# Two attention layers and two feed forward layers on one core: the key matrix's low part in device memory, all key projection units from rounded matmuls

## What is computed

```python
x = x + L0_xattn(layernorm(x), ctx)   # 1024 positions of 128 channels, 64 wide queries and keys
x = x + L0_ffn(layernorm(x))          # 1024 x 1024 matrix of signs, scales from a router of 8
# L1_xattn(layernorm(x), ctx): the one whose keys the change touches
Q = einsum('btx,dx->btd', text, Wq) + bq
K = einsum('bpx,dx->bpd', features, Wk) + bk
scores = einsum('btd,bpd->btp', Q, K) / sqrt(1024)
x = x + softmax(scores) @ features
x = x + L1_ffn(layernorm(x))          # 8 low rank pairs, weighed by a router
```

## Time and profile before

| | |
|---|---|
| median of 3 runs | 2312.98 us (2312.54 to 2313.57) |
| the profiled execution | 2312.58 us |
| its span, first to last instruction | 2310.7 us |
| PE, DVE, ACT, POOL busy | 2193.5, 1872.3, 1116.4, 259.9 us |
| mean granted TensorE clock | 0.981 of full |
| DMA | 115.58 MB, 50 GB/s in the mean |

### The profile page before, as it was taken

The page is one execution under the profiler, slowest core; times in us unless marked ns, Lnnn a source line. Parts: engine busy times, 40 slices in busy tenths (PEclk is TensorE's granted clock), DMA queues, the critical chain, the costliest instruction groups (busy, mean ns, idle before and its releaser), DMA issues.

```text
span 2310.7 us, 34120 instructions
## 1 busy us (share of the span) xinstructions
PE 2193.5 (95%) x11166; PEld 1672.1 (72%) x11166; DVE 1872.3 (81%) x3130; ACT 1116.4 (48%) x1657; POOL 259.9 (11%) x302
## 2 busy tenths in 40 slices
PE   1997999999999999999999999999999999999995
PEld 1785677777777777777777777777777777777764
DVE  1435889888888888988888888888888888898883
ACT  1103455555545545555555555555555554555541
POOL 0000111111111111111111111111111111111100
PEclk7899999999999999999999999999999999999997
DMA  8001111111111111111111111111111111111100
GB/s 243 10 1 46 46 37 55 54 54 36 54 45 45 54 53 37 54 54 38 52 54 45 45 54 36 54 54 54 36 54 45 45 54 54 36 54 54 41 23 28
DMA packets 50217, 115.58 MB, mean 50 GB/s; under 512 B 14800, under 2 KB 23248, under 8 KB 50192
## 3 DMA queue, kind: packets, MB, share of 16 engines
q1 hardware_dynamic: 38624, 113.26, 14.9%
q10 hardware_dynamic: 11568, 1.98, 0.6%
HBM read 81.67 MB, written 16.78 MB: 43 GB/s over the span
## 4 chain that ended last, share of the span: by engine, by line
PE 77%; DVE 9%; issue 3%; ACT 2%; POOL 0%; DMA 0%; DVEq 0%; SPq 0%; POOLq 0%; ACTq 0%
PE acc L1091 15%; PE acc L1052 10%; PE scores L1035 5%; PE shared L1065 5%; PE shared L1066 5%; PE scores L1080 5%; PE scores L1079 5%; PE shared L1015 4%; PE shared L1182 3%; PE shared L1166 3%; PE scores L1193 2%; PE scores L1187 2%; DVE x L813 2%; DVE prob L812 2%; PE acc L1048 2%
## 5 line engine op out<-in xcount | busy, mean ns | idle before, releaser
L903 DVE TENSOR_TENSOR p_lo<-prob,p_hi 128x1024 fp32r<-128x1024 f32 x256 | 312.4, 1220 | 106.3 <-ACT p_hi L709 88.4
L702 ACT ACTIVATE prob<-scores 128x1024 f32<-128x1024 f32 x256 | 260.6, 1018 | 228.9 <-PE scores L1080 177.7
L796 DVE TENSOR_REDUCE neg_max<-scores 128x1 f32<-128x1024 f32 x256 | 312.6, 1221 | 38.7 <-PE scores L1035 33.7
L617 POOL TENSOR_TENSOR rstd<-var_eps,minus_half 128x1 f32<-128x1 f32 x128 | 126.9, 991 | 1865.2 <-DVE var_eps L790 1865.2
L709 ACT ACTIVATE p_hi<-prob 128x1024 fp32r<-128x1024 f32 x256 | 271.4, 1060 | 42.8 <-PE acc L1091 38.6
L1052 PE MATMUL acc<-m_whole,cT_whole 128*128 128x512 f32 x512 | 255.9, 602 | 0.0
L911 DVE TENSOR_TENSOR p_sum<-p_sum,prob 128x1024 f32<-128x1024 f32 x192 | 234.1, 1219 | 0.0
L1065 PE MATMUL shared<-signT,y_hi 128*128 128x512 f32 x512 | 206.1, 403 | 0.4 <-ACT oscale L691 0.4
L1079 PE MATMUL scores<-q_hl,k_hh 128*128 128x512 f32 x512 | 201.4, 393 | 1.8 <-DVE q_m L885 1.4
L1066 PE MATMUL shared<-signT,y_lo 128*128 128x512 f32 x512 | 202.4, 395 | 0.0
L1035 PE MATMUL scores<-k_hh,q_hl 128*128 128x512 f32 x512 | 201.9, 475 | 0.3 <-issue 0.3
(11 more groups left out here) (221 smaller groups left out, 4309.8 us busy)
## 6 DMA issues: line engine op xcount, KB each, us to landing
c_in<-in_ctx SPq DMA_DIRECT2D x32, 512.0 KB, 3.3
xn<-in_x SPq DMA_DIRECT2D x32, 512.0 KB, 4.1
x<-in_x SPq DMA_DIRECT2D x32, 512.0 KB, 3.3
c_val<-in_ctx SPq DMA_DIRECT2D x32, 512.0 KB, 3.5
out_x<-oscale SPq DMA_DIRECT2D x32, 512.0 KB, 2.8
q_m<-q_hl SPq DMA_DIRECT2D x32, 256.0 KB, 3.1
k_hh<-k_hh SPq DMA_DIRECT2D x32, 256.0 KB, 3.4
wq_nat<-in_L_xattn_Wq SPq DMA_DIRECT2D x4, 1024.0 KB, 9.9
```

The lines of the kernel that those rows point to most:

```text
L702: nc.scalar.activation(prob[s % 2][:, :], scores[s % 2][:, :], ACT.Exp).then_inc(exp_ready, 1)
L796: nc.vector.tensor_reduce(neg_max[:, t:t + 1], scores[t % 2][:, :], AX_X, ALU.max, negate=True).then_inc(row_max, 1)
L903: nc.vector.tensor_tensor(p_lo[s % 2][:, :], prob[s % 2][:, :], p_hi[s % 2][:, :].bitcast(F32), ALU.subtract).then_inc(p_lo_ready, 1)
```

## The change

M is held as high and low parts for all 8 tiles. The high part stays in SBUF (m_hi, now 8 tiles). The low part is written to device memory (m_low, 16 pieces of 128 x 512, 256 KB each) during the setup, and in every pass SyncE reads the 16 pieces back into a ring of 8 (m_ring). Every unit is three rounded matmuls, in the order hi x hi, lo x hi, hi x low piece, the last of which waits for its piece; each unit raises kw_unit_done, which frees a slot of the ring and takes the place of kw_done. The context is split in both halves: cT_hi and cT_lo for 8 tiles, cT_whole is gone.

The memory is laid out anew: low parts of tiles 4 to 7 are staged in the not yet written tiles 0 to 3 of m_hi, those of tiles 0 to 3 in m_lo_last, gate_parts shares memory with attn.

The order in a pass changes too: the transposes of c_in stand ahead of weigh_values(7), the transposes of xn_3 ahead of both values; ScalarE makes cT_hi twice, then both norm halves, then both den_rows halves; VectorE makes cT_lo in two halves. On SyncE the pieces 12 to 15 of a and 0 to 7 of b stand ahead of c_in, the pieces 8 to 11 of b ahead of the output store.

```diff
-        m_hi = sb("m_hi", [P, TS, D], F32R)
-        m_whole = sb("m_whole", [P, T - TS, D])
+        m_hi = sb("m_hi", [P, T, D], F32R)
...
-        m_lo = sb("m_lo", [P, TS, D], F32R)
+        with ExitStack() as before:
+            m_lo_last = sb("m_lo_last", [P, TS, D], F32R, before)
+        SLOTS = 8
+        m_ring = sb("m_ring", [P, SLOTS, HALF], F32R)
+        m_low = nc.dram_tensor("m_low", [2 * T, P, HALF], F32, kind="Internal").ap()
...
+            def low_stage(ft, cols):
+                return m_lo_last[:, ft, cols] if ft < TS else m_hi[:, ft - TS, cols]
...
+                    for n, (kind, i) in enumerate(groups):
+                        if kind == "m":
+                            ft, h = f_order[i // 2], i % 2
+                            sp.wait_ge(copied, sum(g[0] != "sign" for g in groups[:n + 1]))
+                            sp.dma_start(m_low[h * T + ft],
+                                         low_stage(ft, slice(h * HALF, (h + 1) * HALF)).bitcast(F32)).then_inc(m_stored[ft], 16)
+                    for ft in range(T):
+                        sp.wait_ge(m_stored[ft], 2 * 16)
...
-                            if ft < TS:
-                                nc.vector.tensor_copy(m_hi[:, ft, cols], s[:, :]).then_inc(m_hi_made, 1)
-                                dve.wait_ge(m_hi_made, 2 * ft + i % 2 + 1)
-                                last = nc.vector.tensor_tensor(m_lo[:, ft, cols], s[:, :], m_hi[:, ft, cols].bitcast(F32), ALU.subtract)
-                            else:
-                                last = nc.vector.tensor_copy(m_whole[:, ft - TS, cols], s[:, :])
+                            if ft < TS and i % 2 == 0:
+                                dve.wait_ge(m_stored[ft + TS], 2 * 16)
+                            nc.vector.tensor_copy(m_hi[:, ft, cols], s[:, :]).then_inc(m_hi_made, 1)
+                            dve.wait_ge(m_hi_made, i + 1)
+                            last = nc.vector.tensor_tensor(low_stage(ft, cols), s[:, :], m_hi[:, ft, cols].bitcast(F32), ALU.subtract)
...
+                def low_unit(u):
+                    sp.dma_start(m_ring[:, u % SLOTS, :].bitcast(F32), m_low[u]).then_inc(m_loaded[u % SLOTS], 16)
...
+                    if attend:
+                        for u in range(12, 16):
+                            sp.wait_ge(kw_unit_done, nth(16, a, u - SLOTS + 1))
+                            low_unit(u)
+                    if prepare:
+                        for u in range(SLOTS):
+                            if attend:
+                                sp.wait_ge(kw_unit_done, nth(16, a, u + SLOTS + 1))
+                            low_unit(u)
...
+                    if prepare:
+                        for u in range(8, 12):
+                            sp.wait_ge(kw_unit_done, nth(16, b, u - SLOTS + 1))
+                            low_unit(u)
...
+                    if prepare:
+                        act.wait_ge(cT_done, nth(2, b, 1))
+                        act.wait_ge(kw_unit_done, nth(16, b - 1, 16))
+                        nc.scalar.activation(tile4(cT_hi, 0), shared[0][:, :], ACT.Identity).then_inc(cT_hi_ready, 1)
+                        act.wait_ge(cT_done, nth(2, b, 2))
+                        nc.scalar.activation(tile4(cT_hi, 1), shared[1][:, :], ACT.Identity).then_inc(cT_hi_ready, 1)
                     if chain:
                         act.wait_ge(den_done, nth(1, a, 1))
                         normalize_half(3, c, 0, xn_3, res)
+                        normalize_half(3, c, 1, xn_3, res)
                     if attend:
                         evict_den(a, 0)
...
-                        dve.wait_ge(cT_hi_ready, nth(1, b, 1))
-                        nc.vector.tensor_tensor(cT_lo[:, :, :].rearrange("p t c -> p (t c)"), shared[0][:, :],
-                                                cT_hi[:, :, :].rearrange("p t c -> p (t c)").bitcast(F32),
-                                                ALU.subtract).then_inc(cT_lo_ready, 1)
+                        for h in range(2):
+                            dve.wait_ge(cT_hi_ready, nth(2, b, h + 1))
+                            nc.vector.tensor_tensor(tile4(cT_lo, h), shared[h][:, :], tile4(cT_hi, h).bitcast(F32),
+                                                    ALU.subtract).then_inc(cT_lo_ready, 1)
...
-                        if f < TS:
-                            mm(acc[:, half(h)], cT_hi[:, f, :], m_hi[:, f, half(h)], start=f == 0, stop=False)
-                            mm(acc[:, half(h)], cT_hi[:, f, :], m_lo[:, f, half(h)], start=False, stop=False)
-                            last = mm(acc[:, half(h)], cT_lo[:, f, :], m_hi[:, f, half(h)], start=False, stop=f == T - 1)
-                        else:
-                            last = mm(acc[:, half(h)], cT_whole[:, f - TS, :], m_whole[:, f - TS, half(h)],
-                                      start=f == 0, stop=f == T - 1)
-                        if f == T - 1:
-                            last.then_inc(kw_done, 1)
+                        mm(acc[:, half(h)], cT_hi[:, f, :], m_hi[:, f, half(h)], start=f == 0, stop=False)
+                        mm(acc[:, half(h)], cT_lo[:, f, :], m_hi[:, f, half(h)], start=False, stop=False)
+                        pe.wait_ge(m_loaded[u % SLOTS], nth(32, a, 16 * (u // SLOTS + 1)))
+                        mm(acc[:, half(h)], cT_hi[:, f, :], m_ring[:, u % SLOTS, :], start=False,
+                           stop=f == T - 1).then_inc(kw_unit_done, 1)
...
+                        if prepare and s == 7:
+                            for h in range(2):
+                                pe.wait_ge(x3_ready, nth(2, c, h + 1))
+                                transposes(h, c_in, cT_done)
                         if attend:
                             weigh_values(a, s)
...
-                    if prepare:
+                    if chain:
                         for h in range(2):
-                            pe.wait_ge(x3_ready, nth(2, c, h + 1))
-                            transposes(h, c_in, cT_done)
+                            pe.wait_ge(normed[3], nth(2, c, h + 1))
+                            pe.wait_ge(cT_lo_ready, nth(2, b, h + 1))
+                            transposes(h, xn_3, xnT_done[3])
                     if prepare:
                         pe.wait_ge(normed[0], nth(1, b, 1))
                         values(0, a)
-                    if chain:
-                        for h in range(2):
-                            pe.wait_ge(normed[3], nth(2, c, h + 1))
-                            pe.wait_ge((cT_lo_ready, cT_whole_ready)[h], nth(1, b, 1))
-                            transposes(h, xn_3, xnT_done[3])
-                    if prepare:
                         values(1, a)
```

More of the change, by code:

```diff
@@ L87, in build @@
             wf_first = sb("wf_first", [P, TS, D], F32, before)
-        m_hi = sb("m_hi", [P, TS, D], F32R)
-        m_whole = sb("m_whole", [P, T - TS, D])
-        wf_last = m_whole
+            wf_last = sb("wf_last", [P, T - TS, D], F32, before)
+        m_hi = sb("m_hi", [P, T, D], F32R)
         with ExitStack() as before:
@@ L156, in build @@
             b_hi_made = sem("b_hi_made", tmp)
+            m_stored = [sem(f"m_stored{i}", tmp) for i in range(T)]
+            def low_stage(ft, cols):
+                return m_lo_last[:, ft, cols] if ft < TS else m_hi[:, ft - TS, cols]
             groups = ([("sign", i) for i in range(T)] + [("low", 0), ("low", 1), ("b", 0), ("b", 1)]
@@ L404, in build @@
         k_l1 = sb("k_l1", [P, D], F32R)
-        cT_hi = sb("cT_hi", [P, TS, P], F32R)
-        cT_lo = sb("cT_lo", [P, TS, P], F32R)
-        cT_whole = sb("cT_whole", [P, T - TS, P])
+        cT_hi = sb("cT_hi", [P, T, P], F32R)
+        cT_lo = sb("cT_lo", [P, T, P], F32R)
         neg_max = sb("neg_max", [P, T])
@@ L449, in build @@
         attn = sb("attn", [P, P])
+        gate_parts = attn
         attnT = sb("attnT", [P, P])
@@ L479, in build @@
         maxscores_done = sem("maxscores_done")
-        kw_done = sem("kw_done")
+        kw_unit_done = sem("kw_unit_done")
+        m_loaded = [sem(f"m_loaded{i}") for i in range(SLOTS)]
         max_turned = sem("max_turned")
@@ L503, in build @@
         cT_lo_ready = sem("cT_lo_ready")
-        cT_whole_ready = sem("cT_whole_ready")
         k_hi_ready = sem("k_hi_ready")
@@ L678, in body @@
                     if attend:
-                        act.wait_ge(kw_done, nth(2, a, 1))
+                        act.wait_ge(kw_unit_done, nth(16, a, 8))
                         act.wait_ge(biased, nth(1, a - 1, 1))
@@ L737, in body @@
                         normalize_half(3, c, 0, xn_3, res)
+                        normalize_half(3, c, 1, xn_3, res)
                     if attend:
                         evict_den(a, 0)
-                    if prepare:
-                        act.wait_ge(cT_done, nth(2, b, 1))
-                        act.wait_ge(kw_done, nth(2, b - 1, 2))
```

(9 more changed lines are left out.)

9 lines of the change are left out of this document (3 added, 6 removed).

## The result

The changed kernel takes 2287.32 us (median of four, 2286.79 to 2289.61); the kernel before, run beside it, takes 2313.28 (2312.54 to 2315.55). The ratio is 0.9888, 95% interval 0.9872 to 0.9904. The forecast was 2288. The profiled execution was the longest of the four, 2289.61 us with a span of 2287.8, against 2312.58 and 2310.7 before.

A forecast was written before the change was run, and what follows sets the result against it. TensorE was taken to set most of the period, VectorE to bound wherever it never idles. 2312.6 - 29.0 (31 x 0.49 + 30 x 0.46) - 1.8 (period 1) + 6.3 (start) = 2288 us; range 2270 to 2306.

The forecast's parts named there:

- Units 5 to 7, 0.49 us: Maximum stage: these three rewritten units, 0.163 us each, bring VectorE's row maxima forward, gaining 0.49 us per period.
- Units 4 and 12 to 15, nothing: Maximum stage: 0.82 us of TensorE saved per period behind a busy VectorE becomes waiting and gains nothing.
- Rival A: All TensorE savings count, 1.31 us per period, because VectorE follows; 2263 us, chance 0.07.
- Handover, 0.46 us: End of a period: the new orders let VectorE's x1_half start earlier, gaining 0.46 us in each of 30 periods.
- B: Handover brings nothing: ScalarE's queue is later than worked out and x1_half stays put; 2302 us, chance 0.14.
- C: Neither gain shows and only the start is paid; 2317 us, about no change, chance 0.05.
- D: Handover gets later as work put ahead on ScalarE delays x1_half; 2323 us at 0.7 us later, chance 0.06.
- The cover of the added subtraction: Handover: VectorE's second cT_lo hides in 1.39 us of vanishing idle time; uncovered it would cost 0.69 us per period.
- Transfers, waits and increments, nothing: Every period: 4.2 MB more reads, added waits and unit increments cost 0; other end for waits 0.3 us per period.
- E: The 4.2 MB more per period written into SBUF slow TensorE's matmuls; 2328 us at 2%, chance 0.03.
- G: Pieces arrive late and units wait for them; 2350 us at 2 us late, chance 0.02.
- F: Added waits and increments on TensorE cost their bound, 0.3 us per period; 2297 us, chance 0.05.

The follow-up runs named there:

- full_567: Changed kernel with units 5, 6 and 7 each as one full-precision matmul of the high parts, low parts left out; 2304.25 us, ratio 0.9971.
- Full_rest: Changed kernel with units 4 and 12 to 15 each as one full-precision matmul of the high parts, low parts left out; 2293.76 us, ratio 0.9921.
- experiment 4: Two variants of the changed kernel: units 14 and 15 alone, or 4, 12 and 13 alone, as one full-precision matmul each; 2288.91 and 2290.22 us.
- order_only: Kernel before with only the new handover orders on TensorE and ScalarE; units, memory and transfers as before; 2301.54 us, ratio 0.9957.
- old_order: Changed kernel with the handover orders of the kernel before on TensorE and ScalarE; 2336.97 us, ratio 1.011.
- after_again: Changed kernel, unchanged, run again on the chip of no_pieces and late_start; 2289.13 us, ratio 0.9899.
- no_pieces: Changed kernel without piece loads or their waits, the third matmul reading the high part instead; 2281.14 us, ratio 0.9862.
- late_start: Changed kernel with the first eight pieces issued behind the first c_in and xn, not ahead; 2281.92 us, ratio 0.9867.
- full_4_12_13: Changed kernel with units 4, 12 and 13 each as one full-precision matmul of the high parts, low parts left out; 2290.22 us, ratio 0.9905.
- den_between: late_start with ScalarE copying the first denominator half between the two norm halves, not behind both; 2274.67 us, ratio 0.9833.

## Why the prediction was right, and where its terms were off

- **Units 5 to 7, 0.49 us: right.** full_567 gives 0.49, and the price of a unit, 0.163 us, with it. One thing expected of the profile was not so: the idle time before r_max shrank to 0.20 us and did not go.
- **Units 4 and 12 to 15, nothing: mis-sized, 0.15 us per period, 4.6 us.** The step that failed is "From 1039.71 on it never idles. So units 12 to 15 ... bring nothing". That VectorE never idles shows that nothing holds it up. It does not show that nothing else ends later. The rows that say so, the transpose of the maxima 1.71 us behind the start of TensorE's last two units and with no wait before it, were in the trace of before. Full_rest showed it, and experiment 4 that no one group of units does it: TensorE had 0.33 us to spare at the stage's end, and with all five it is 0.2 us over. Rival A, all 0.82 us, is refuted by the same run.
- **Handover, 0.46 us: right in kind, mis-sized, 0.37** (order_only). The step was the denominators' copy from 1018.12 + 2 x 0.70 = 1019.52, 4.79 us behind the sums of before (1014.73). In after it starts at 1012.68, 4.92 us behind them. The sum left out that the norm halves stand behind the second context copy: they start 3.49 us behind the sums, and the prediction had them at the shift, 3.39 behind. The chain ScalarE, denominators, x1_half is the one that was named; it is 0.1 us longer, and VectorE idles 0.33 us for it. Rivals B, C and D, no gain or a loss here, did not come: order_only gains by itself. That a later step on ScalarE delays x1_half and with it the period, as D has it, old_order shows: 1.17 us against before.
- **The cover of the added subtraction: right, its price wrong.** It is hidden behind the 1.39 us. I put 0.69 us as the price without the cover; old_order lost 1.17 against before, because the second subtraction also waits 0.49 us for a second copy on ScalarE. An added instruction brings its inputs' waits with it.
- **Transfers, waits and increments, nothing: right.** No instruction of TensorE waits for a piece in after. The period is the same with the pieces and their waits (63.55, after_again) and without both (63.55, no_pieces); so E, and G with it, are refuted, and of F the half that is the added wait. The increment on each unit stays in no_pieces and in every variant of after, so it was not taken away by itself. What bounds it is the sum: its cost would be what the parts give (0.37 against before, 0.49 and 0.15 against after: 1.01) less the 1.00 found, 0.01 us, if the parts add up, and that is no more than the readings are good for. From the first to the last maximum full_567, with an increment and a wait on each of these units, takes no longer than order_only with none (13.24 and 13.25 us; unit 4, 0.163 us cheaper in full_567, also differs). And in after, with a wait and an increment on each unit, five matmuls pass from 1036.76 to 1037.93 at 0.234 us each, as against 0.233. The Trainium skill, "TensorE: Matmul & The Clock Gate", section "The cost: per-tile semaphore tail", gives about 26 ns for each further increment in a group of tiles. Carried over to 14 more increments per period, that is an estimated 0.37 us; no such cost shows here.

```profile
1036.76 0.40 PE L1070 MATMUL acc<-m_hi,cT_hi 128*128 128x512 f32 x1
...
1037.93 0.39 PE L1073 MATMUL acc<-m_ring,cT_hi 128*128 128x512 f32 x1
```

- **Start, 6.3 us: mis-sized, 7.8 at the first unit.** The first issue is 0.3 us later (182.94 against 182.63), the number that was worked out, but no run shows its reason: late_start has the same setup and issues at 182.57, full_4_12_13 at 181.08. The statistics are 194.51 - 187.17 = 7.3 us later; from the first issue they are 11.57 us and not 4.54, so the eight pieces cost 7.0 us. That was the upper end, from the pace of c_in and xn themselves; I had taken 5.3 from the fastest stretch of the setup. The second subtraction costs 0.5, not 0.7: 2.68 us of wait at the first unit against 2.19.
- **Period 1, 1.8 us: right, 1.6.** The last four maxima of period 1 start at 213.56 in after and 207.89 before, 5.7 us later, the first of its eight at 206.80 and 200.52, 6.3 us later, and the first maximum of period 2 at 261.07 and 256.42, 4.65 us later: 6.3 - 4.65 = 1.6.

The sum of the spans by these readings: +7.8 at the first unit; -1.5 from there to the first maxima (6.3), for a reason told below; -1.6 to period 2 (4.65); -29.9 in the 30 periods that follow (25.2 us earlier, at 2168.27 against 2193.49); +2.3 from there to the end of the profiled execution: -22.9. The forecast had -29.0 - 1.8 + 6.3 = -24.5. It came out right partly because errors cancelled: 4.6 us more from units 4 and 12 to 15 against 2.7 less from the handover, and a start dearer by 1.5 against a clock that came back earlier by 1.5. For the +2.3 at the end the forecast has no term; this last stretch takes 117.2 us in before, 119.6 in after, and between 116.9 and 121.5 in the traces of the variants, so it says little about the change. Of the mechanisms, the two gains and the start were named rightly and one part of the maximum stage was missed; the agreement to 1 us is luck.

## What to carry to other kernels

An engine that never idles bounds a stage only if what follows it waits for it: read the instruction behind the stage's end. If it has no wait before it, its own engine may have been the last, and how far it starts behind its engine's instruction before it and behind the other engine's last one shows whether it was. When an operand is split, put the steps that make it in the order of their consumers as part of the same change; here all of the change but the orders lost 1%, and with them it won 1%. Issue what is needed first ahead of the rest: eight pieces in front of the first inputs cost 7 us, and their price was that of 2.1 MB at the pace of the transfers beside them, not at that of the best stretch of the trace.

## What was not expected of the hardware

TensorE's granted clock falls to the lower level, 1.2 GHz, in stretches at the start and at the end, where TensorE has gaps, and not in the same places from trace to trace. Behind the first unit (stretches; columns as above), before and after:

```profile
197.00:203.00 6.00, 6.00 (x18) 4.01 (x16) 3.35 (x4) 0.00 (x0) 0.00 (x0) 0.73 0.46 165
```

```profile
190.00:203.20 13.20, 7.23 (x28) 4.65 (x28) 4.55 (x11) 5.86 (x9) 0.74 (x2) 0.70 0.36 120
203.20:211.00 7.80, 7.74 (x33) 6.31 (x34) 6.21 (x8) 0.53 (x2) 0.00 (x0) 1.00 0.74 227
```

In before the clock was low just as the first units ran; in after it had been low ahead of them and was at its upper level when they came. From the first unit to the first maximum pass 5.08 us in before and 3.54 in after. That is the 1.5 us, and no gain of the change itself. The same kernel in after_again takes 5.09, with its first units at a lower clock,

```profile
203.20:211.00 7.80, 7.80 (x28) 6.18 (x27) 4.66 (x7) 0.00 (x0) 0.00 (x0) 0.78 0.65 173
```

and wins it back by the first maximum of period 2, since the clock of after falls once more before it (0.57 of full between 249 and 253 us, behind 3.4 us of which it was busy 2.84; 1.00 in after_again): that maximum comes at 260.65, in after at 261.07. late_start has its first units at 0.73 again,

```profile
197.00:203.00 6.00, 6.00 (x21) 4.74 (x21) 3.51 (x5) 0.00 (x0) 0.00 (x0) 0.73 0.57 172
```

and keeps its 0.55 us of delay from the first unit (195.99) to the first maxima (201.08 against 200.52). In the last stretch it went the other way, 30 us of it in before and in after:

```profile
2250.00:2280.00 30.00, 18.35 (x83) 13.09 (x83) 13.47 (x37) 6.78 (x14) 3.83 (x5) 0.84 0.10 35
```

```profile
2225.00:2255.00 30.00, 20.40 (x83) 14.76 (x82) 13.35 (x37) 5.54 (x13) 3.51 (x4) 0.76 0.10 36
```

83 matmul records were busy 20.40 us and not 18.35, at 0.76 and not 0.84. After's three other executions are 1.9 to 2.8 us shorter than the profiled one, and such a stretch would account for them, but they have no trace, so that stays open. It is also why the period, and not the total, was compared.

Two smaller ones. The 512 transfers of a piece landed 2.4 to 5.8 us after their issue, median 3.1, while the period moved 115 GB/s in place of 49, and TensorE's pace did not change. And in den_between a step of 0.25 us on VectorE gave 0.22 us of period while TensorE, busy for over 98% of it, took on a wait of 0.59: full as it looks by its share, TensorE has stretches in every period in which it isn't the bound.
